# One megakernel (deformable convolution, causal attention, expert routing): own step tables for the first and last images, image 0 raised without a DMA, projections on two row halves, the causal mask added by one product

## The reference, cut to what matters

```python
x = x + deform_conv(_gn(x), kernel, bias, offset_w, offset_b)   # 3x3, learned shifts, 4-point sampling
t = _to_tokens(x)                                               # 8 x 1024 x 64
t = t + attention(_ln_t(t), Wq, bq, Wk, bk, Wv, bv)             # causal, one head of 64
...
# routing: logits = norm(t) @ gate_w.T + gate_b, softmax over the tokens, the best 8 tokens of each
# of 32 experts, a two-layer MLP (64 -> 256 -> 64, gelu) for each expert, scattered back and added
```

## Time and profile before

| | |
|---|---|
| median of 3 runs | 536.76 us (536.1 to 539.37) |
| profiled execution | 543.43 us, its span 541.6 us |
| TensorE busy | 435.6 us, 80% of the span |
| VectorE, ScalarE, GpSimd busy | 325.3, 298.0, 152.0 us |
| moved by DMA | 75.82 MB, mean 140 GB/s |

### The profile page before, as it was taken

The page is one execution under the profiler, slowest core; times in us unless marked ns, Lnnn a source line. Parts: engine busy times, 40 slices in busy tenths (PEclk is TensorE's granted clock), DMA queues, the critical chain, the costliest instruction groups (busy, mean ns, idle before and its releaser), DMA issues. The chain is left out here.

```text
span 541.6 us, 13979 instructions
## 1 busy us (share of the span) xinstructions
PE 435.6 (80%) x5841; PEld 320.4 (59%) x5841; DVE 325.3 (60%) x478; ACT 298.0 (55%) x544; POOL 152.0 (28%) x121
## 2 busy tenths in 40 slices
PE   1316897799999999999999999998996678317485
PEld 0102674477777677777767767775774556317264
DVE  2215676677887788788778878868757423204034
ACT  1113563767777777777777777777664435012200
POOL 4130018006334612633451263405124020211000
PEclk9955698799999999999999999999999857755579
DMA  9359979966787787677878767875800000009307
GB/s 224 78 131 234 210 190 203 205 155 139 171 191 168 171 191 179 143 169 179 177 171 201 186 135 171 186 171 131 198 11 1 1 9 4 1 13 212 133 2 155
DMA packets 33645, 75.82 MB, mean 140 GB/s; under 512 B 22312, under 2 KB 25257, under 8 KB 27241
## 3 DMA queue, kind: packets, MB, share of 16 engines
q1 hardware_dynamic: 28698, 72.90, 58.5%
q10 hardware_dynamic: 4880, 1.98, 1.4%
HBM read 64.70 MB, written 7.01 MB: 132 GB/s over the span
## 5 line engine op out<-in xcount | busy, mean ns | idle before, releaser
L823 DVE TENSOR_TENSOR wring<-stage 96x640 f32<-96x640 f32 x192 | 158.4, 864 | 30.9 <-ACT stage L639 27.5
L995 PE MATMUL psum<-wring,zring 96*64 96x160 f32 (+4 forms) x1728 | 130.2, 295 | 7.3 <-DVE wring L823 7.3
L995 PEld LDWEIGHTS psum<-wring,zring 96*64 96x64 f32 x1728 | 106.0, 141 | 27.4 <-issue 24.0
L785 DVE TENSOR_REDUCE negmax<-psum 128x1 f32<-128x128 f32 (+3 forms) x64 | 48.5, 757 | 65.9 <-PE psum L848 65.8
L962 PE MATMUL psum<-kern,img 64*32 64x192 f32 x1536 | 59.6, 348 | 13.8 <-ACT zring L646 13.6
L646 ACT ACTIVATE zring<-psum 96x768 f32<-96x768 f32 x64 | 51.4, 802 | 26.4 <-PE psum L962 24.9
L672 ACT ACTIVATE pT<-psum 128x512 f32<-128x512 f32 (+2 forms) x96 | 46.5, 485 | 28.6 <-PE psum L856 27.6
L856 PE MATMUL psum<-const,prob 128*128 128x128 f32 x288 | 55.2, 306 | 7.9 <-ACT pT L672 5.5
L720 ACT ACTIVATE prob<-psum,negmax 128x128 f32<-128x128 f32 (+3 forms) x64 | 47.0, 734 | 16.5 <-DVE negmax L785 16.4
L843 PE MATMUL psum<-kT,qT 64*128 64x128 f32 (+4 forms) x400 | 51.9, 363 | 4.5 <-DVE kT L781 3.0
L636 ACT ACTIVATE stage<-stage,const 96x384 f32<-96x384 f32 x64 | 38.9, 608 | 25.4 <-DMA stage<-near 25.3
(11 more groups left out here) (116 smaller groups left out, 533.6 us busy)
## 6 DMA issues: line engine op xcount, KB each, us to landing
stage<-near SPq DMA_DIRECT2D x192, 288.0 KB, 5.7
w<-in_w SPq DMA_DIRECT2D x1, 2080.0 KB
tok<-in_x SPq DMA_DIRECT2D x8, 256.0 KB, 5.2
img<-img SPq DMA_DIRECT2D x8, 256.0 KB, 3.0
images<-img SPq DMA_DIRECT2D x8, 256.0 KB, 3.8
w<-in_w SPq DMA_DIRECT2D x1, 2048.0 KB
near<-tents SPq DMA_DIRECT2D x32, 45.0 KB
shifts<-offT SPq DMA_DIRECT2D x8, 128.0 KB, 5.9
```

What stands on the lines that cost most here:

```text
L785: dve.tensor_reduce(negmax[:, t:t + 1], score_rows(t, a), AX.XY, ALU.max, negate=True).then_inc(s["mx"], 1)
L823: dve.tensor_tensor(rows[:, ky, :, place], stage[0:KX, q % STG, ky, 1:, :], stage[0:KX, q % STG, ky, 0, :].unsqueeze(1).to_broadcast([KX, ...
L995: ins = pe.matmul(psum[C * e:C * e + C, 2 + half, (lo % 16) * W:(lo % 16 + n) * W], zring[0:KX, q % ZRING, i % 2 * 2 + e, ky * C:(ky + 1) ...
```

## The change

1. The step tables become four sets, chosen by image (`KIND_OF_IMAGE`): one for image 0, one for images 1 to 5, one for image 6 and one for image 7. STEPS becomes 944, so the numbers are finer. The order of the queues changes in many places. On TensorE: in the start, `mix0`, `mix1` and `mix2` of image 0 now stand ahead of `turn.1` and `groups.1`, and `offsets.1` after `pair3.0`. On SyncE, `second.1` now comes after `load4.0` and no longer after `load2.0`. For every middle image `project` stands ahead of `out` of the image before, and `value2` ahead of `prob10`. At the end, `project.7` stands ahead of `value3.6` and `out.6`, scores 0 to 3 of image 7 stand ahead of its first `prob`, `norm2.6` and `gate.6` stand after `score5.7`, and `value1` to `value3` of image 7 are spread among the `prob` steps. The routing steps of the first four images on VectorE move behind the maximum of image 6's last score row; only the first of them stays ahead.
2. Image 0 is raised without a DMA. ScalarE and VectorE copy its channels out of PSUM a second time, to rows 64 to 127 of `img` (`keep_twin`), the group sums are made on both halves, and VectorE normalises both halves (`normalise_first`) in place of GpSimd. TensorE's `offsets.0` waits for these and not for the DMA.
3. `keep_channels` makes one copy of 128 partitions x 512 in place of two of 64 x 512. The projection is one product of 64 rows on each row half, in separate banks, and the bias is added in the copies of q and k (`query`, `key`), which put the tokens in order. The gate does the same in 8 products of 128 columns, where there were 4 of 256.
4. The mask is one product over 128 rows.
5. The tents' DMAs count in four semaphores, so that `load0` waits for the first two of the eight DMAs alone. ScalarE waits for the first constants and copies the identity to bf16 ahead of its first step.

```diff
-STEPS, ROUND = 80, 242
-PE_AT = dict(
...
+STEPS, ROUND = 944, 4881
+KIND_OF_IMAGE = [0, 1, 1, 1, 1, 1, 2, 3]
+PE_AT = (
...
+def table(tables, image):
+    return tables[KIND_OF_IMAGE[image] if isinstance(image, int) else 1]
...
         sync.wait_ge(self.s["pn"], b + 1)
-        sync.dma_start(self.img[C:P, b % 2, HALO - 1:HALO - 1 + H, :], self.rows(b)).then_inc(self.s_up[b % 2], 16)
+        if b > 0:
+            sync.dma_start(self.twin(b), self.rows(b)).then_inc(self.s_up[b % 2], 16)
...
+    def tents_kept(self, eng, b, j):
+        eng.wait_ge(self.s_near[j], 16 * 2 * (b + 1))
...
+        if b == 0:
+            ins.then_inc(self.s["first"], 1)
+            if h == 0:
+                self.keep_twin(eng, h)
...
+    def keep_twin(self, eng, h):
+        src = self.psum[C * h:C * h + C, 0, :].rearrange("c (q n) -> c q n", n=P)
+        if h == 0:
+            eng.activation(self.half_rows(self.twin(0), h), src, ACT.Copy).then_inc(self.s["raw_lo"], 1)
+        else:
+            eng.tensor_copy(self.half_rows(self.twin(0), h), src).then_inc(self.s["raw_hi"], 1)
...
+    def normalise_first(self, dve):
+        gs = self.gs
+        dve.wait_ge(self.s["raw_lo"], 1)
+        dve.wait_ge(self.s["raw_hi"], 1)
+        dve.wait_ge(self.s["rstd"], 1)
+        dve.tensor_scalar(self.rows(0), self.rows(0), gs[0:C, 0:1], gs[0:C, 4:5],
+                          ALU.subtract, ALU.mult).then_inc(self.s["pn"], 1)
+        dve.tensor_scalar(self.twin(0), self.twin(0), gs[C:P, 0:1], gs[C:P, 4:5],
+                          ALU.subtract, ALU.mult).then_inc(self.s["up0"], 1)
...
-            if p == 0:
-                prep.tents_kept(sync, b)
+            if p % 2 == 0:
+                prep.tents_kept(sync, b, p // 2)
...
         def keep_channels(act, done):
-            blocks = lnT[0:C, :].rearrange("c (q h p) -> c q h p", h=2, p=P)
-            for h in range(2):
-                ins = act.activation(blocks[:, :, h, :], psum[C * h:C * h + C, 4, :].rearrange("c (q p) -> c q p", p=P),
-                                     ACT.Copy)
-            ins.then_inc(done, 1)
+            act.activation(channels[:, :], psum[:, 4, :], ACT.Copy).then_inc(done, 1)
...
-                    act.activation(qT[C * h:C * h + C, :], wide(0, a)[0:C, :], ACT.Copy, scale=scale).then_inc(s["q_sb"], 1)
+                    act.activation(by_token(qT[C * h:C * h + C, :]), by_half(psum[0:C, 4:6, :]), ACT.Identity,
+                                   bias=qbias[:, 0:1], scale=scale).then_inc(s["q_sb"], 1)
...
-                dve.tensor_copy(kT[C:P, :], psum[C:P, 4:6, :].rearrange("c a q -> c (a q)")).then_inc(s["k_sb"], 1)
-                dve.tensor_copy(kT[0:C, 0:HB], psum[C:P, 4, :]).then_inc(s["k_sb"], 1)
+                dve.tensor_scalar(by_token(kT[C:P, :]), by_half(psum[C:P, 4:6, :]), kbias[C:P, 2:3], None,
+                                  ALU.add).then_inc(s["k_sb"], 1)
+                dve.tensor_scalar(by_token(kT[0:C, 0:HB]), by_half(psum[C:P, 4:6, 0:HB // 2]), kbias[C:P, 2:3], None,
+                                  ALU.add).then_inc(s["k_sb"], 1)
...
-            for h in range(2):
-                ins = pe.matmul(psum[:, score_bank(t, a) + (0 if t == 0 else 1), half - P:half], exact[C:P, h, 0, :],
-                                exact[C:P, h, 1, :], start=False, stop=(h == 1))
+            ins = pe.matmul(psum[:, score_bank(t, a) + (0 if t == 0 else 1), half - P:half], exact[:, 0, :], exact[:, 1, :],
+                            start=False, stop=True)
...
-                    ins = pe.matmul(psum[:, 4 + h, :], wqk[:, :], lnT[:, h * HB:(h + 1) * HB],
+                    ins = pe.matmul(psum[:, 4 + h, :], wqk[C * h:C * h + C, :], channels[C * h:C * h + C, :],
                                     start=True, stop=True)
...
                 for j in range(4):
-                    ins = pe.matmul(psum[E * j:E * j + E, 4, 0:T // 4], gate[:, :], lnT[:, j * (T // 4):(j + 1) * (T // 4)],
-                                    start=True, stop=True)
+                    for h in range(2):
+                        ins = pe.matmul(psum[E * j:E * j + E, 4 + h, 0:P], gate[C * h:C * h + C, :],
+                                        channels[C * h:C * h + C, j * P:(j + 1) * P], start=True, stop=True)
```

More of the change, by code:

```diff
@@ L39 @@
 REACH = 5
-STEPS, ROUND = 80, 242
-PE_AT = dict(
-    turn=[-140],
-    groups=[-133],
-    offsets=[-117],
-    mix=[-50, -47, -40, -30, 3, 7, 10, 15],
-    pair=[-33, -32, -27, -25, 1, 5, 6, 9, 13, 14, 18, 22, 23, 25, 28, 29],
-    back=[35],
-    norm=[52],
-    project=[84],
-    score=[88, 91, 96, 106, 112, 116, 121, 125],
-    prob=[92, 97, 111, 114, 117, 119, 122, 124, 126, 129, 131, 134],
-    value=[99, 118, 136, 160],
-    out=[162],
-    norm2=[181],
-    gate=[184])
-ACT_AT = dict(
-    raw=[-147],
-    leave=[-127],
-    tent=[-116, -114],
-    columns=[-63, -58, -50, -45, -37, 0, 5, 9],
-    rows=[-60, -55, -51, -38, 1, 3, 6, 10],
-    half=[15, 19],
-    norm=[40],
-    query=[82],
-    exp=[84, 88, 92, 98, 103, 107, 112, 117],
-    prob=[87, 91, 101, 104, 106, 108, 111, 114, 116, 118, 119, 121],
-    out=[125],
-    norm2=[174],
-    logits=[176])
@@ new lines @@
+POOL_AT = (
+    dict(
+        normalise=[-3791],
+        centre=[1],
+        norm=[65],
+        centre2=[1009],
+        norm2=[1873]),
+    dict(
+        normalise=[-1888],
+        centre=[16],
+        norm=[32],
+        centre2=[992],
+        norm2=[1008]),
+    dict(
+        normalise=[-1887],
+        centre=[1],
+        norm=[17],
+        centre2=[1953],
+        norm2=[2881]),
+    dict(
+        normalise=[-2767],
+        centre=[65],
+        norm=[929],
+        centre2=[5729],
+        norm2=[15089]))
@@ new lines @@
+SP_AT = (
+    dict(
+        second=[-6479],
+        tents=[-6463],
+        load=[-2767, -1743, 49, 145, 1921, 1953, 2017, 2018],
+        logits=[4849]),
+    dict(
+        second=[992],
+        tents=[1088],
+        load=[1888, 1904, 1920, 1952, 1968, 1984, 2000, 2016],
+        logits=[4880]),
+    dict(
+        second=[977],
+        tents=[1089],
+        load=[1921, 1922, 2001, 2033, 2865, 2866, 2867, 2868],
+        logits=[5697]),
+    dict(
+        second=[1058],
+        tents=[1937],
+        load=[2001, 2002, 2003, 2004, 2849, 2865, 2945, 2946],
+        logits=[11489]))
@@ L105, in constants @@
+DVE_CHOICE = [1953, 2561, 2945, 3377, 5777]
+ACT_CHOICE = 1441
 def constants():
@@ L351, in distances @@
         if b > 0:
-            self.tents_kept(dve, b - 1)
+            for j in range(4):
+                self.tents_kept(dve, b - 1, j)
         dve.wait_ge(self.s["off_sb"], b + 1)
```

577 lines of the change are left out of this document (381 added, 196 removed).

## The result

| | before | after |
|---|---|---|
| median, same chip, 4 runs each | 538.07 us (536.1 to 539.78) | 506.79 us (505.68 to 516.54) |
| profiled execution (before: the one in front of the prediction), its span | 543.43, 541.6 us | 507.9, 506.1 us |
| TensorE, VectorE, GpSimd busy | 435.6, 325.3, 152.0 us | 416.1, 345.3, 159.5 us |

The ratio is 0.9413 (95% interval 0.9356 to 0.947): 31.3 us less, where 24 were forecast.

A forecast was written before the change was run, and what follows sets the result against it. The prediction took a chain then transfers to bound the start, TensorE the middle, and a chain of copies, maxima and exponentials the last image; 6 + 8 + 10 = 24 us off 536.8 gives 513 us, range 501 to 528.

The forecast's parts named there:

- Start, 6 us: Start of the kernel: offsets 6 us earlier, first loads 7 us earlier, of which 6 us carried out; bounds 1 and 11.
- Projection, 0.95: Each middle image: two products on two row halves overlap, 0.96 us for 1.91; gain 0.95, or 0 without overlap.
- Mask, 0.05 each, 0.4 an image: Middle images: one product of 128 rows for two gains 0 to 0.1 us, taken as 0.05, eight times an image.
- Gate, 0: Middle images: eight products of half the width hold the same columns in twice the instructions; 0, with 0.2 either way.
- Middle, 8: Images 0 to 5: 1.35 us less per image, six times, 8 us in all, between 1 and 12.
- Into the scores of image 7, 5: Last image: 3 us of waiting for copies of q and k, 2 us from later routing; 5 us, between 2 and 7.
- Inside, 4: Within the last image: TensorE idle time goes at the same clock; 4 us, between 0 and 4.5.
- What the edits do in the last block, 0.6: End of the last image: the channel copy in one part, no longer two, 0.6 us.
- gain only in the middle: Rival: transfers and `offsets.1` pace the start, TensorE's low clock the last image; 13 us less, 524 us; chance 0.2.
- no overlap: Rival: projection halves don't overlap and the mask drains; middle gives 0, start and end 16, so 521 us; chance 0.05.
- the clock stays up: Rival: clock stays up in the last image, idle time at 80 to 100 us closes; 503 us; chance 0.08.
- slower case: Rival: second norm reaches TensorE late in every middle image; 6 us late gives 543 us; chance 0.07.

The follow-up runs named there:

- second profile: The unchanged changed kernel run again, on the chip of three other follow-ups: 0.9445 times the kernel before.
- old tables: Changed kernel's code with the step tables of the kernel before for every image, so the edits without the new order: 0.9683 times the kernel before.
- experiment 4: Changed kernel with the causal mask added by two products of 64 rows, as before: 0.9443 times the kernel before.
- new tables alone: Kernel before with all step tables of the changed kernel, so the new order without the edits: 0.9909 times the kernel before.
- experiment 10: Kernel before with VectorE's routing of the first four images behind image 6's last maximum, nothing else changed: 1.001 times the kernel before.
- `norm2.6` ahead: Changed kernel with image 6's second norm and gate ahead of image 7's fourth row of scores: 0.9488 times the kernel before.
- middle table: Changed kernel with images 6 and 7 on the middle images' step table, routing after image 6's last maximum: 0.9528 times the kernel before.
- image 0 by DMA: Changed kernel with image 0 normalised by GpSimd and raised to the second half by a DMA, as before: 0.9458 times the kernel before.
- experiment 5: Changed kernel with both projection products on rows 0 to 63, which changes the output: 0.9504 times the kernel before.
- experiment 11: Changed kernel with GpSimd adding the values' bias to only the first of eight token blocks: 0.9422 times the kernel before.

## Why the prediction was right, and where its sizes were off

The measured 506.8 us lies in the forecast's range, 501 to 528, 6 us below its 513. The mechanisms of the start and of the projection were those that the traces show; in the last image two terms came out near their size or above it by other parts than those worked out, and that is partly luck.

- **Start, 6 us.** Offsets 5.6 us earlier, first load 7.0, first piece 7.9, as worked out. The step was right that not all of it arrives. Image 1's first load went out at 68.09 us (66.15 in the second profile), for 65 to 67 worked out. With the old tables it went out at 64.52, so the holding back is the own table's work; but `back.1` was no earlier there (119.67), so that image 1's tents set the end of its convolution isn't shown. What the step missed is the clock. Before, TensorE was busy all the time from 100 to 120 us at 0.74. The kernel before with its routing moved has the same start but a clock of 1.00 there, and its `back.1` is at 125.92 instead of 128.98: by this pair of profiles some 3 of the 8.2 us are the clock and some 5 the edits. The kernel with the mask in two had 0.76 there, and its `back.1` came at 126.62, 7.6 us after that of the changed kernel's second profile. The times bear it out: the three profiled executions with 0.72 to 0.76 there were the slowest of their kernels (543.43 for 536.1 to 539.78 in the table above; 516.11 for 509.04 to 513.82 with the mask in two; 516.92 for 507.23 to 510.37 with the short bias), and that of the kernel before with its routing moved, at 1.00, its fastest. So it differs from execution to execution, by some 3 to 8 us on top of the order.
- **Projection, 0.95.** 0.85 to 0.95, and shown to be the overlap of the halves.
- **Mask, 0.05 each, 0.4 an image.** 0.1 to 0.2 an image at the steps, gains and losses mixed. The Trainium skill's rule that a change of mode drains the engine (TensorEngine Tiling (Array Packing), Key Properties) was the better guide for the sign where 64-row products follow; the price of a change, some 0.07 us by experiment 4, is small.
- **Gate, 0.** Gained 0.19: twice the instructions on two halves were still the shorter.
- **Middle, 8.** Steps of 0.95 + 0.15 + 0.2 = 1.3 us, nearly the forecast's 1.35 by other parts; but a middle image is 1.1 shorter with the new order (0.9 in the second profile), and 0.74 with the old. The stretch of the table above still lost 9.9 us, since it isn't six equal images: 4.8 of them lie between `back.1` and `project.1` (23.19 before, 18.36 after). The new tables alone have 18.45 there and the old tables with the edits 23.08, so this part is the order's and was in no term. Of the 1.3 us of a middle image the rest went into waits of TensorE, from 150 to 310 us 2.8 us for weights and copies of probabilities where the kernel before had 1.4 in all.
- **Into the scores of image 7, 5.** Measured 8.5: 4.0 up to image 6's last transposes (2 forecast), 4.5 from there to the first score (3 forecast). For the first part, the routing moved by itself (experiment 10) has 12.9 us up to the last transposes, for 15.2 before and 11.2 in the changed kernel. In the second part the weak step is "I take 3 us off (the wait)". The wait of 2.97 us didn't go, it became 1.17. What left the chain to the first score is this: 1.5 us with 22 of the 52 value products, which now stand ahead of the transposes, and the copy behind them; 1.0 with `out`, which runs beside the copies of q; the projection's own 0.9; 0.45 of transposes that ran at a clock of 0.63 before and at 1.00 after; and 0.5 in the copies of q and k. The prediction also has the value products beside the copies of q and k; only the copies of k ran there (VectorE, 402.94 to 405.0). It also read the old projection as one "at the low clock": the clock was 1.00 there, and the row is as long as in the middle (1.98).
- **Inside, 4.** Measured 5.8 (30.88 for 25.10), but by another part. The step said that what can go is idle time, at the same clock. Idle time gave 1.6 us. The other 4.1 are the clock, which the prediction had only in a rival: 26.09 us of work at 0.67 is 17.5 at 1.00, and 21.95 at 0.80 is 17.6, so the work didn't change. That the term came out near its size is luck. Unlike the clock of the start, this one repeats: 0.79 or 0.80 in eight of the nine profiles with the edits and the changed tables of images 6 and 7, and 0.77 in the ninth, `norm2.6` ahead; 0.72 with the middle table there, 0.75 with the old tables, 0.71 in the kernel before with its routing moved, 0.87 with the new tables only. What in the order sets it isn't shown.
- **What the edits do in the last block, 0.6.** Only the channel copy had been counted. The projection is 0.9 us shorter as well, the last gate 0.4 (1.14 to 0.78), the channel copy of image 6 0.7. The gate of image 6 took 1.01 us (442.12 to 443.13) at a clock of 0.50 and now 0.39 (420.88 to 421.27) at 1.00, so not all of its 0.6 is the edit. These do not explain the 3.6 us of the kernel with old tables. Up to its first score that kernel is 0.3 us longer than before (26.56 for 26.29): the wait for the copies is 4.10 for 2.97, and the projection's gain is lost in it. Between the first score and `out` it is 3.3 shorter, and 3.1 of these are work that took 23.03 us at 0.75 for 26.09 at 0.67. The last 0.6 are the channel copy and what follows `out`, as forecast.
- **After the block, 0.** 2.5 us less, but 1.5 of it lies between the last logits and the routing (8.0 us before, 6.5 after), and the kernel with image 0 by DMA, which has the changed kernel's code there, took 8.8. So it isn't the change's.

The rival "gain only in the middle" (524) fell with the last image, "no overlap" (521) with experiment 5. Of "the clock stays up" (503) half came true: from `back.7` to the last gate the mean clock was 0.83 for 0.76. By two of the prediction's own signs something was wrong with it: TensorE shows waits inside the middle (2.8 us of 160), and the clock of the last image wasn't 0.67. The slower case didn't occur: `norm2` waited for 0.3 us in a middle image of the changed kernel. Moved ahead in the last image, it showed its price at once.

## What to carry to other kernels

Where engines run their queues in order, follow the whole chain again after a step has moved, on every engine, with work, idle time and clock apart. The wait that was to go stayed in part, and more than its length left the chain by other ways; and the copy of q, which the move was meant to bring forward, stood behind another copy on ScalarE and lost 2.5 us. No experiment moved it, so what it would give is open. A step table of its own for an image isn't worth the same everywhere: for the last two images it gave 8.9 us of the block, 4 to 6 of them in the time, for the first it likely cost some. And before an order is changed for a stretch, look at the granted clock of the stretch in more than one profile, since a nearly equal kernel may have it at 0.76 or at 1.00.

## What the runs showed of the hardware

**Large products of VectorE and GpSimd hold each other up.** The changed kernel's weights (VectorE, a product of two operands in SBUF) have a mean of 943 ns for 864, and single ones take twice their usual 0.81 us (two engines of one stretch):

```profile
305.75 1.04 POOL L1543 TENSOR_TENSOR an_tmp<-tok,an_small 128x512 f32<-128x512 f32 x1 [2.66 <-DVE an_small L1529]
306.88 1.50 POOL L1545 TENSOR_TENSOR an_tmp<-an_tmp 128x512 f32<-128x512 f32 x1
```

```profile
305.82 1.65 DVE L1073 TENSOR_TENSOR wring<-stage 96x640 f32<-96x640 f32 x1 [0.28 <-issue]
...
308.44 0.81 DVE L1073 TENSOR_TENSOR wring<-stage 96x640 f32<-96x640 f32 x1
```

The weight that began 0.07 us after GpSimd's product shows 1.65 us, as if it waited for its end (306.79) and then took its time; GpSimd's next, begun beside it, shows 1.50 for its usual 1.04. All weights of the changed kernel say the same. Of its 192, 96 had no GpSimd instruction beside them and took 0.76 to 0.82 us each. The 33 that took over 1.0 us all ran beside a GpSimd TENSOR_TENSOR of 128x512. Beside GpSimd's TENSOR_SCALAR of 64x1024 (3.79 us) 13 weights took 0.82 in the mean, and beside its operations on 128x8 the mean was 0.81: those don't hold it up. In the kernel before 15 weights took over 1.0 us, again all beside a TENSOR_TENSOR of 128x512. With the old tables the mean is 865 ns in the middle, so it is the order that puts the two side by side. The Trainium skill has this as an exclusive lock for an operation of VectorE with two inputs in SBUF against one of GpSimd that reads SBUF (SBUF — State Buffer, Who interferes with whom); the trace agrees for the products of 128x512, and shows no lock beside the TENSOR_SCALAR, which reads SBUF too. It cost no time that experiment 11 could find: VectorE is idle for 3 of 40 us in the middle.

**The clock of the start differs from run to run.** From 100 to 120 us the clock was 1.00 in both profiles of the changed kernel and 0.76 in the one with the mask in two, whose queues differ there by the masks alone (the copies that prepare them lie in the first 20 us):

```profile
100.00:120.00 20.00, 20.00 (x254) 15.44 (x256) 11.45 (x18) 10.33 (x20) 0.00 (x0) 0.76 0.79 172
```

TensorE was never idle in these 20 us, made 254 products where the changed kernel made 318, and GpSimd, which waits for the others there, did nothing. In slices of 5 us, the changed kernel's second profile has its low stretch at 80 to 85 us (0.50, with 3.54 us of work in 5) and is at 1.00 from 90 us on. The kernel with the mask in two has that one as well (0.50 at 80 to 85 us), and a second from 95 to 110 us (0.50, 0.50, 0.53), in which TensorE worked all the time; ahead of it, from 90 to 95 us, it had worked 3.53 us at 0.77, and the other 3.80 at 1.00. The two differ already at 60 to 65 us (1.00 and 0.50). What decides is open. But the first low stretch lies where TensorE waits for others anyway, and the second where it has work for every us, and that one delays all that follows.
